# The first cross attention in pairs of heads, with the rounding of probabilities and queries on GpSimd

## What is computed

```python
def _fq_sym(x, axis):
    s = jnp.maximum(jnp.max(jnp.abs(x), axis=axis, keepdims=True) / 127.0, 1e-08)
    return jnp.clip(jnp.round(x / s), -127.0, 127.0) * s
def _fq_unsigned(x, axis):
    s = jnp.maximum(jnp.max(x, axis=axis, keepdims=True) / 255.0, 1e-08)
    return jnp.clip(jnp.round(x / s), 0.0, 255.0) * s
q = (x @ Wq + bq).reshape(1, B * N, H, hd)
kv = (cond @ Wkv + bkv).reshape(1, -1, 2, H, hd)
q, k, v = _fq_sym(q * scale, axis=-1), _fq_sym(k, axis=-1), _fq_sym(v, axis=2)   # v: over all keys
attn = _fq_unsigned(softmax(einsum('bhqd,bhkd->bhqk', q, k)), axis=-1)
out = einsum('bhqk,bhkd->bhqd', attn, v).reshape(B, N, C) @ Wp + bp
```

## Time and profile before

| | |
|---|---|
| median of 3 runs | 4110.76 us (4109.12 to 4114.24) |
| profiled execution | 4110.44 us, span 4108.4 us |
| busy over the span | PE 81%, PEld 59%, DVE 68%, ACT 48%, POOL 10% |
| the stage that is changed | from 274.4 to 776.8 us of the span |

### The profile page before, as it was taken

One profiled execution on the slowest core, in us unless ns is written; L12 is line 12 of the kernel. 1 busy time (PEld: TensorE's weight loads), 2 busy tenths in 40 slices (PEclk: granted clock), 3 DMA queues, 4 the chain that ended last, 5 costly groups with the idle time before them and its releaser, 6 DMA issues. The chain is left out here.

```text
span 4108.4 us, 59566 instructions
## 1 busy us (share of the span) xinstructions
PE 3335.9 (81%) x18333; PEld 2417.8 (59%) x18364; DVE 2798.4 (68%) x8822; ACT 1969.4 (48%) x5854; POOL 407.3 (10%) x495
## 2 busy tenths in 40 slices
PE   7967888697999999674569976559999999999565
PEld 5644545474777777463237764227777777777344
DVE  4667888537788887566964437866666666666597
ACT  4537888414555555123521112336666666666243
POOL 0000000001111110110111100001111111111100
PEclk9986666799999999876569988569999999999588
DMA  1000000100000000000000012000000000000000
GB/s 55 2 23 1 1 1 1 80 1 13 1 1 1 1 1 1 39 1 29 1 15 1 1 43 100 1 11 1 1 1 1 1 1 1 1 1 1 32 1 21
DMA packets 6585, 50.37 MB, mean 12 GB/s; under 512 B 256, under 2 KB 4480, under 8 KB 4608
## 3 DMA queue, kind: packets, MB, share of 16 engines
q1 hardware_dynamic: 6272, 46.57, 2.9%
...
## 5 line engine op out<-in xcount | busy, mean ns | idle before, releaser
L2162 DVE CUSTOM_DVE_ANT_0 L3A_masked<-ps,L3A_hidden,L3A_negrstd 128x128 f32<-128x128 f32 (+1 forms) x512 | 193.5, 415 | 324.7 <-PE ps L2053 235.0
L2111 ACT ACTIVATE L3A_probs<-L3A_masked,L3A_negmax 128x128 f32<-128x128 f32 (+1 forms) x512 | 228.6, 449 | 238.2 <-DVE L3A_negmax L2162 238.2
L331 PE MATMUL ps<-s_weights_b,s_XT 128*128 128x512 f32 (+1 forms) x648 | 302.5, 596 | 24.7 <-ACT L1A_qn L1969 9.1
L2081 PE MATMUL ps<-s_weights_b,L3A_OT 128*128 128x256 f32 x1024 | 265.7, 382 | 14.8 <-DVE s_R L2191 14.8
L331 PE MATMUL ps<-s_weights_b,s_Xc 128*128 128x512 f32 x512 | 244.2, 599 | 7.8 <-DVE L3A_rot L2026 3.3
L877 ACT ACTIVATE L0X_pf<-ps,L0X_negmax_scaled,L0X_qscale 128x512 f32<-128x512 f32 x256 | 209.4, 818 | 54.8 <-DVE L0X_negmax_scaled L923 53.5
L2034 POOL TENSOR_TENSOR L3A_rstd<-L3A_ve,s_mhalf 128x4 f32<-128x4 f32 x144 | 145.1, 1008 | 854.4 <-DVE L3A_ve L1994 854.4
L918 DVE TENSOR_REDUCE L0X_negmax<-ps 128x1 f32<-128x512 f32 x256 | 176.4, 689 | 55.4 <-PE ps L816 47.3
L2081 PEld LDWEIGHTS ps<-s_weights_b,L3A_OT 128*128 128x128 f32 x1024 | 175.7, 192 | 29.2 <-issue 15.9
L868 ACT ACTIVATE L0X_pT<-ps,L0X_less 128x512 bf16<-128x512 f16 x256 | 184.9, 723 | 9.7 <-PE ps L825 9.6
L331 PEld LDWEIGHTS ps<-s_weights_b,s_XT 128*128 128x128 f32 x648 | 124.4, 211 | 109.0 <-issue 68.1
(11 more groups left out here) (512 smaller groups left out, 9038.7 us busy)
## 6 DMA issues: line engine op xcount, KB each, us to landing
...
```

The lines of the kernel that those rows point to most:

```text
L331: last = pe.matmul(out, lhs(k), rhs(k), start=(k == 0), stop=(k == n - 1))
L2081: last = pe.matmul(c.bank(3)[:, j * DM:(j + 1) * DM], OT[:, u % 4, j * P:(j + 1) * P], w["wo"][:, h, :], start=(h == 0 and j == 0), stop=( ...
L2111: last = a.activation(pr[:, u % 4, cols], ms[:, u % 2, cols], ACT.Exp, bias=nmx[:, h, j:j + 1], scale=-1.0, accum_out=sm[:, h, j:j + 1])
L2162: last = eng.tensor_tensor_reduce(out=ms[:, u % 2, cols], in0=s[:, cols], in1=hidden[:, P - j * P:2 * P], scale=-1.0 if gated else nrs[:, ...
```

## The change

The whole stage is one block, and its unit is a pair of heads of a token tile: 128 pairs p in slots of one pair each (`SLOTS`), 16 for each sequence, and 16 slots more in which the last sequence is finished.

- Scores of a pair go to two banks next to each other (0 and 1, or 2 and 3). One reduction gives both maxima; two small operations multiply with the query scale and add ln 255, so the exponential comes out times 255. The row sums are then times 255 as well, so the factor 1/255 is gone.
- The rounding of a pair (1,024 columns) is one instruction on GpSimd: add and subtract 12582912 (`MAGIC`), result in bf16. `ph` has 4 buffers.
- Eight transposes of a pair go to one bank (4 or 5) as bf16. They are copied by ScalarE for even pairs and by VectorE for odd ones.
- Side steps on TensorE are X, Q, T0, T1, oT and Y, one each in slots 0, 1, 6, 7, 9 and 10 of a sequence, all through bank 7 in a fixed order (`STEP_AT`, `pe_side`); the output projection and the query projection are one step each.
- VectorE takes the maxima and scales of the queries (both token tiles at once); GpSimd multiplies, rounds and writes the three parts (`pool_q`). GpSimd also adds the output bias to X beforehand (`Xb`).
- Value scales are multiplied once into the rows of the output weights `wp`, so `VS` and its products go. Values are rounded partly on ScalarE. In the preparation GpSimd splits the keys into their parts.

The diff, cut. Of the removed lines, those that are not shown are the functions `steps`, `outputs`, `take`, `scores`, `turn`, `values` and the loops around them, which are printed above.

```diff
+    PAIRS = TT * HEADS // 2
+    U = SEQS * PAIRS
+    SLOTS = range(U + PAIRS)
+    LN255 = float(np.log(255.0))
+    TURN_LAG, VALUE_LAG = 3, 5
+    STEP_AT = {0: ("X", 1), 1: ("Q", 1), 6: ("T0", 1), 7: ("T1", 1), 9: ("oT", -1), 10: ("Y", -1)}
+    steps = [("X", 0), ("Q", 0), ("T0", 0), ("T1", 0)]
+    step_at = {}
+    for s in SLOTS:
+        if s % PAIRS in STEP_AT:
+            what, ahead = STEP_AT[s % PAIRS]
+            i = s // PAIRS + ahead
+            if 0 <= i < SEQS:
+                step_at[s] = (what, i)
+                steps.append((what, i))
...
+        kx = c.oT
+        tmp = S.sb("tmp", [P, TT, DM])
+        am, inv = (S.sb(x, [P, 2 * HEADS]) for x in ("am", "inv"))
+        qs = S.sb("qscale", [P, 2, 2 * HEADS])
+        ks = S.sb("kscale", [P, 2, HEADS])
...
+        pf = S.sb("pf", [P, 3, 2, KEYS])
+        ph = S.sb("ph", [P, 4, 2, KEYS], BF16)
+        pT = S.sb("pT", [P, 3, 2, KEYS], BF16)
+        nmx, nms = (S.sb(x, [P, 4, 2]) for x in ("negmax", "bias"))
+        sm = S.sb("sums", [P, 2, 2 * HEADS])
+        ri = S.sb("rsums", [P, 2 * HEADS])
...
+        def pe_side(pe, x):
+            what, i = x
+            m = number[x]
+            if m:
+                pe.wait_ge(side_act, act_through(steps[m - 1]))
+                pe.wait_ge(side_vec, vec_through(steps[m - 1]))
...
+            if what == "Q":
+                if i:
+                    e.wait_ge(q_parts, TT * i)
+                v(e.tensor_tensor(row[:], halves, over(w["bq"], TT), ALU.add), side_vec)
+                v(e.tensor_reduce(am[:], heads_of(flat(row[:]), 2 * HEADS), AX.X, ALU.max, apply_absolute_value=True))
+                v(e.tensor_scalar(qs[:, i % 2, :], am[:], DH ** -0.5 / 127.0, 1e-8, ALU.mult, ALU.max))
+                v(e.reciprocal(inv[:], qs[:, i % 2, :]))
+                v(e.tensor_scalar(inv[:], inv[:], DH ** -0.5, None, ALU.mult), q_scaled)
+            else:
+                e.wait_ge(xb_ready, i + 1)
+                v(e.tensor_tensor(c.R[:], Xb[:], halves, ALU.add), side_vec)
+                S.vec_norm_stats(v)
+        def pool_q(p, i):
+            g = p.eng
+            g.wait_ge(q_scaled, i + 1)
+            if i:
+                g.wait_ge(side_made, number["T1", i - 1] + 1)
+            else:
+                g.wait_ge(k_turned, KT)
+            p(g.tensor_tensor(heads_of(flat(tmp[:]), 2 * HEADS), heads_of(flat(row[:]), 2 * HEADS), spread(inv[:], DH), ALU.mult))
+            p(g.tensor_scalar(tmp[:], tmp[:], MAGIC, MAGIC, ALU.add, ALU.subtract))
+            for j in range(TT):
+                for part in range(3):
+                    p(g.tensor_copy(parts(j)[:, part], heads_of(tmp[:, j, :])), q_parts if part == 2 else None, free=True)
...
+                def scores(p):
+                    b, j, m = place(p)
+                    if p == 0:
+                        pe.wait_ge(kT_ready, KT)
+                        pe.wait_ge(v_ready, KT)
+                    if p % PAIRS == 0:
+                        pe.wait_ge(side_act, act_through(("T1", b)))
+                    if p >= 2:
+                        pe.wait_ge(exp_ready, p - 1)
+                    for x in range(2):
+                        r = slice(ROWS * x, ROWS * x + ROWS)
+                        last = pe.matmul(c.bank(2 * (p % 2) + x), qT[r, b % 2, m, j * P:(j + 1) * P], kT[r, m, :], start=True, stop=True)
+                    last.then_inc(scores_made, 1)
+                def turn(p):
+                    pe.wait_ge(steps_ready, p + 1)
+                    if p >= 2:
+                        if by_vec(p - 2):
+                            pe.wait_ge(vec_turned, vec_turns(p - 2))
+                        else:
+                            pe.wait_ge(act_turned, act_turns(p - 2))
+                    o = c.bank(4 + p % 2, BF16)
+                    for x in range(2):
+                        for t in range(KT):
+                            last = pe.transpose(o[:, x * KEYS + t * P:x * KEYS + (t + 1) * P], ph[:, p % 4, x, t * P:(t + 1) * P], c.idb[:])
+                    last.then_inc(turned, 1)
+                def values(p):
+                    b, j, m = place(p)
+                    if by_vec(p):
+                        pe.wait_ge(vec_turned, vec_turns(p))
+                    else:
+                        pe.wait_ge(act_turned, act_turns(p))
+                    if b and p % PAIRS == 0:
+                        pe.wait_ge(o_read, b)
+                    for x in range(2):
+                        h = 2 * m + x
+                        for t in range(KT):
+                            last = pe.matmul(c.bank(6)[:, j * DM + h * DH:j * DM + (h + 1) * DH], pT[:, p % 3, x, t * P:(t + 1) * P],
+                                             V[:, t, h * DH:(h + 1) * DH], start=(t == 0), stop=(t == KT - 1))
+                    last.then_inc(o_made, 1)
...
+                def exps(p):
+                    b, j, m = place(p)
+                    a.wait_ge(max_ready, p + 1)
+                    if p >= 3:
+                        a.wait_ge(steps_ready, p - 2)
+                    for x in range(2):
+                        at = j * HEADS + 2 * m + x
+                        last = a.activation(pf[:, p % 3, x, :], c.bank(2 * (p % 2) + x), ACT.Exp, scale=qs[:, b % 2, at:at + 1],
+                                            bias=nms[:, p % 4, x:x + 1], accum_out=sm[:, b % 2, at:at + 1])
+                    last.then_inc(exp_ready, 1)
+                def take(p):
+                    a.wait_ge(turned, p + 1)
+                    if p >= 3:
+                        a.wait_ge(o_made, p - 2)
+                    a.copy(flat(pT[:, p % 3]), c.bank(4 + p % 2, BF16)).then_inc(act_turned, 1)
+                a.wait_ge(S.loaded, 16)
+                for f in range(KC):
+                    a.wait_ge(v_made, f + 1)
+                    a.activation(vT[:, f, :], c.bank(4 + f), ACT.Identity, bias=w["bv"][:, f:f + 1]).then_inc(vT_ready, 1)
+                act_side(a, steps[0])
+                for f in range(KC):
+                    a.wait_ge(v_scaled, f + 1)
+                    a.activation(vT[:, f, :], vT[:, f, :], ACT.Identity, bias=c.magic[:, 0:1], scale=vsc[:, f, 2:3]).then_inc(v_round, 1)
...
+                def maxima(p):
+                    b, j, m = place(p)
+                    eng.wait_ge(scores_made, p + 1)
+                    v(eng.tensor_reduce(nmx[:, p % 4, :], c.ps[:, 2 * (p % 2):2 * (p % 2) + 2, :], AX.X, ALU.max, negate=True))
+                    for x in range(2):
+                        at = j * HEADS + 2 * m + x
+                        v(eng.tensor_scalar(nms[:, p % 4, x:x + 1], nmx[:, p % 4, x:x + 1], qs[:, b % 2, at:at + 1], LN255,
+                                            ALU.mult, ALU.add), max_ready if x else None, free=True)
+                def take(p):
+                    eng.wait_ge(turned, p + 1)
+                    if p >= 3:
+                        eng.wait_ge(o_made, p - 2)
+                    v(eng.tensor_copy(flat(pT[:, p % 3]), c.bank(4 + p % 2, BF16)), vec_turned, free=True)
+                def outputs(b):
+                    eng.wait_ge(exp_ready, PAIRS * (b + 1))
+                    v(eng.reciprocal(ri[:], sm[:, b % 2]))
+                    eng.wait_ge(o_made, PAIRS * (b + 1))
+                    if b:
+                        eng.wait_ge(side_act, act_through(("oT", b - 1)))
+                    v(eng.tensor_tensor(heads_of(flat(c.On[:]), 2 * HEADS), heads_of(c.bank(6), 2 * HEADS), spread(ri[:], DH), ALU.mult), o_read)
+                    eng.sem_inc(S.on_ready, 1)
...
+                for f in range(KC):
+                    eng.wait_ge(vT_ready, f + 1)
+                    a_, s_, i_ = (vsc[:, f, x:x + 1] for x in range(3))
+                    v(eng.tensor_reduce(a_, vT[:, f, :], AX.X, ALU.max, apply_absolute_value=True))
+                    v(eng.tensor_scalar(s_, a_, 1.0 / 127.0, 1e-8, ALU.mult, ALU.max))
+                    v(eng.reciprocal(i_, s_), v_scaled)
+                vec_side(v, steps[1])
+                for f in range(KC):
+                    v(eng.tensor_scalar(w["wp"][:, f, :], w["wp"][:, f, :], vsc[:, f, 1:2], None, ALU.mult))
+                for t in range(0, KT, 2):
+                    eng.wait_ge(v_turned, t // 2 + 1)
+                    v(eng.tensor_scalar(flat(V[:, t:t + 2, :]), c.bank(2 + t // 2), MAGIC, None, ALU.subtract), v_ready)
+                    eng.sem_inc(v_ready, 1)
...
+                def steps_of(u):
+                    g.wait_ge(exp_ready, u + 1)
+                    if u >= 4:
+                        g.wait_ge(turned, u - 3)
+                    p(g.tensor_scalar(ph[:, u % 4], pf[:, u % 3], MAGIC, MAGIC, ALU.add, ALU.subtract), steps_ready, free=True)
+                p(g.memset(rq[:], 0.0))
+                for t in range(KT):
+                    x = kx[:, t % 2, :]
+                    g.wait_ge(k_rows, t + 1)
                     if t >= 2:
-                        eng.wait_ge(turned, t - 1)
```

(52 more changed lines are left out.)

316 lines of the change are left out of this document (121 added, 195 removed).

## The result

The changed kernel takes 4167.52 us (median of 4 runs, 4165.36 to 4170.6); the kernel before took 4112.5 beside it (4109.12 to 4114.76). The ratio is 1.0135, 95% interval 1.0117 to 1.0153: slower, where 4008 had been forecast. 0.2% is about 8 us.

A forecast was written before the change was run, and what follows sets the result against it. No engine was full; ScalarE set the pace in quiet stretches. Preparation 26.5, loop 356 and tail 17 make 399.5 us against 502.4, a gain of 102.9 from 4110.4, so 4008 us; range 3960 to 4062.

The forecast's parts named there:

- the price of GpSimd's rounding: GpSimd's step over 1,024 columns a pair: 1.3 us taken, between 1.04 and 2.54; 27 us a sequence, hidden behind VectorE.
- rival (a): GpSimd rounds at its two-input rate, 2.54 us a step: 50.5 us a sequence with waits, 4060 us; chance 0.20.
- Rival (d): GpSimd's rounding step is slow: even at 3.2 us a step, about 4215 us at 4.0; chance 0.05.
- the likeliest case's own range: Kernel time of the forecast by itself, from 3985 to 4035 us; chance 0.50.
- Preparation: Stage start to first scores: 26.5 us, with GpSimd making key parts and doing the query work.
- Loop: Eight sequences of 16 pairs: 44.5 us each, 356 us in all.
- The prediction's own walk: Following slots 9 to 11 of the loop with the new prices: 44 us a sequence at 2.4 GHz, 48 at 1.2.
- VectorE's copy: Copy of bf16 from PSUM for every second pair: 1.22 us taken, 0.69 if two columns a cycle.
- the 30 us that the prediction hung on this: With VectorE's copy at two columns a cycle, 34.4 us a sequence for VectorE and a forecast some 30 us lower.
- the next exponentials come 4 to 5 us late after the output projection: In the loop, delay behind the output projection, a single 3.47 us step on TensorE at 1.2 GHz.
- The wait for GpSimd's roundings: In the loop, later pairs' roundings behind the query work: charged nothing; without cover at most 2.7 us a sequence, 22 us.
- Tail: From the last rounding to the next stage: 17.0 us rather than 19.9.

The follow-up runs named there:

- forms: Changed kernel plus 40 GpSimd instructions over 1,024 columns, four of each kind; add-then-subtract took 3.63 us, multiply-then-add 1.05, one operation with a constant 2.77.
- mult_add: Changed kernel with GpSimd's rounding as multiply by 1.0, add 1024 into float16, the copies taking 1024 off; 4030.47 us, ratio 0.9803.
- heads_apart: `mult_add` with two maxima of 512 columns instead of one of 1,024, each exponential waiting for its own; 4025.18 us, ratio 0.9783.
- split_only: `mult_add` with each projection in two halves in neighbouring slots, query transpositions and GpSimd's query work one slot later; 4027.75 us, ratio 0.979.

## Why the prediction was wrong

**The step that failed** is the price of GpSimd's rounding: "I take 1.3", with 2.54 as the upper bound. It takes 3.63. The bounds were a copy over the same 1,024 columns and twice an addition of two tensors over 512; the choice near the copy rested on "it reads one tensor as the copy does". `forms` shows that this is no measure: an add and a subtract of constants cost 3.63, an add of two tensors 2.34, so the upper bound lay below the truth and rival (a) with it. The trace of before has no TENSOR_SCALAR on GpSimd at all, and an operation that no row shows had no right to an upper end built from another kind.

With the true price the prediction's own working names the mechanism. Rival (d), given 0.05, puts the break-even at 3.2 us a step, and its sum for a sequence, 16 x 3.63 + 6.4 = 64.5 us, is what each of the six inner sequences takes. (The query work takes 1.06 + 1.92 + 2.13 us, the bias addition 1.09, the root 0.72, in all 6.9 for 6.4; the rounding of the queries in it, taken at 0.7, was mis-priced by the same step.) The time comes out too: the line from 3.2 us (even) to 4.0 (4215) gives 4110.8 + 0.43 / 0.8 x 104 = 4167 at 3.63, measured 4167.5. That hit is luck in part. The loop took 504 us for the 516 of eight full sequences, since the first and the last are short, and preparation and tail 55 for 43.5; the two errors cancel.

**The rest of the forecast** can be read in `mult_add`, whose step is 1.05: 4030 us at a ratio of 0.9803, inside the likeliest case's own range, 22 us above the 4008. The stage takes 419.0 us against 399.5:

- Preparation 29.5 to the first scores, against 26.5. GpSimd's part of it, in order of time, is shown below: its key parts end at 297.26, 18.6 us after the stage's start where 17.0 was taken (four tiles in 13.6 for 12), and the query work takes 5.3 us from 299.33 for 4.4.
- Loop 369.9 us from the first scores on against 356, 46.2 us a sequence for 44.5. The prediction's own walk gave 44 us at 2.4 GHz and 48 at 1.2 and took 44.5; the clock granted in the loop was 0.68, about a third of the time at 2.4 GHz, at which the walk gives 46.6. The prices on ScalarE, 281.4 / 8 = 35.2 us a sequence for 34.9, and the score matmuls in twos were right. VectorE's copy was taken twice too dear, the scalings too cheap (0.34 for 0.14 + 0.04): 275.1 / 8 = 34.4 us for 38.5. By the Trainium skill's rule of two 2-byte elements at a time (PSUM — Partial Sum Buffer, "Specifications (TRN2)") the copy was to be the cheap one, and the trace agrees, with 0.68 us. That the sum by it, 34.4 us, is met to the tenth is luck: the scalings are dearer and the first and last sequence lighter, an inner one has 35.3. The loop did not get the 30 us that the prediction hung on this, though VectorE was busy no more than 275 of its 370 us.
- Most of what is lost more than forecast lies at the output projection: for "the next exponentials come 4 to 5 us late after the output projection" the pair behind it comes 5.5 us late on average (7.5 for 2.0), VectorE's addition and statistics going ahead of the maximum, and the pair before it 1.0 us late. After the query projection it is 4.3 us for the 3 to 4.5 forecast.
- The wait for GpSimd's roundings, put at nothing, is small: TensorE waits for the step 36 times, 17.4 us in all, and the runs don't show how much of it the stage feels.
- Tail 19.6 against 17.0: the last two pairs' transposes and values run one behind the other at 1.2 GHz, and the end from the transposition of the outputs takes 697.68 - 684.30 = 13.4 us for 11.9.

```profile
283.62 0.40 POOL L996 CAST L0X_rq<-s_oT 128x256 bf16<-128x256 f32 x1 [3.00 <-DVE s_oT L950]
...
296.86 0.40 POOL L996 CAST L0X_rq<-s_oT 128x256 bf16<-128x256 f32 x1
299.33 1.06 POOL L785 TENSOR_TENSOR L0X_tmp<-L0X_row,L0X_inv 128x512 f32<-128x512 f32 x1 [2.07 <-PE ps L708]
300.48 1.94 POOL L786 TENSOR_SCALAR L0X_tmp<-L0X_tmp 128x512 f32<-128x512 f32 x1
302.49 2.13 POOL L789 CAST L0X_rq<-L0X_tmp 128x256 bf16<-128x256 f32 x6
...
684.30 1.08 PE L739 MATMUL ps<-s_const,s_On 128*128 128x128 f32 x4 [0.99 <-DVEq L940]
...
697.68 0.33 SPq L2982 DMA_DIRECT2D s_weights_b<-w_L1A  x1
```

The gain of the rest of the change is real, then: some 80 us in `mult_add`, of which the preparation makes 18 and the loop 64; the changed kernel gives it up, and 55 more, for one choice of operations. The Trainium skill's warning (GPSIMD Engine Reference, "4.1 Engine selection") pointed the right way and was weighed too lightly; the part of it that was leaned on, near line rate with one input, the trace shows for a copy, a cast and a multiply-then-add (1.04 to 1.05 us), not for an addition or a multiplication by a constant (2.77).

What stays open: why `heads_apart` and `split_only` gain so little by themselves and more together, and what a VectorE that is really relieved would bring in the old order. GpSimd's work beside VectorE is no part of it in `mult_add`: over the loop VectorE's instructions are in all 4 us longer than if each had its group's shortest time.
